# A two-layer graph network on one core: node tables laid out by group, query rows scattered by group during the clearing of their table

## The chip, the cores and the metric

The kernel runs on one core of one Trainium2 chip. The metric is device time in microseconds (us) of that core, the median of several runs. A profile is one more execution, recorded by the hardware profiler; its span goes from the first to the last instruction.

## What is computed

12500 nodes with 128 features, 200000 edges sorted by destination. The first layer is an attention layer over edges, the second a sum over neighbours with a small network. Cut to what matters (q, k, v have 8 heads of 16; every node also has a loop to itself):

```python
h = relu(layernorm(x))
q, k, v = (layernorm(h) @ W + b for each of q, k, v)
e = sum(q[dst] * k[src]) / sqrt(16)            # per edge and head, and per loop
alpha = softmax of e over the edges of a node
att = segment_sum(alpha * v[src], dst); 0 where a node has no edge
x1 = h + att @ Wo + bo;  x = x + x1 + gelu(layernorm(x1) @ W1 + bf1) @ W2 + bf2
h = relu(layernorm(x))
x = x + relu(((1 + eps) * h + segment_sum(h[src], dst)) @ gW1 + gb1) @ gW2 + gb2
```

## The kernel before

Five engines run programs written out by hand, with semaphores between them. Nodes are held in SBUF as `nodes`, 128 partitions by 98 columns; partition p has the nodes 98p to 98p+97. The work on nodes goes through 14 groups of 7 columns (`G`), two groups in each iteration of a loop (`PAIRS` = 7). Edges are held as 128 chunks of 1568 steps, handled in 98 batches of 16 steps (`B`); partition p walks through the edges 1568p to 1568p+1567.

*Stage A* (`group_a` on PE, DVE, ACT, `search` on GpSimd) normalizes each group, projects q, k and v (`take_qkv`, L1347 and L1348, adds the bias out of PSUM: k and v to a buffer that goes to the DRAM table `kv_tab`, q back into `nodes`), multiplies q by k for the loop scores (`loop_products`, L1353; `loop_scores`, L1360), and looks for the last edge of every node: a count over sampled destinations gives a block of 32 edges, GpSimd gathers that block (7 gathers per group from `dst_tab`, L612), and `last_edges` counts in it. GpSimd also adds a bias to the residual rows (L795) for the table `h0_tab`.

*The query table.* `q_edges` has a row of 128 values for each edge position. It is cleared to zero with 98 writes of 1 MB (`zero_fill`, L504, on SyncE's queue, two in flight). Then the query of each node is scattered to the row of its first edge, 98 scatters of 128 rows on GpSimd (`scatter_q`, L616); a node without edges gets an index out of bounds and is skipped. Each scatter reads a copy that ScalarE makes (`copy_q`, L978, L979). In stage B a scan on DVE (`fill`, L1459) carries each query down to the other edges of its node.

*Starts.* The index of a node's first edge is the last edge of the node before it, plus one. The node before lies mostly in the column before, but for the first column in another partition, so last edges are stored to `last_tab` in DRAM and read back shifted by one (L960, L963, L1424 to L1427). Two gathers from `last_tab` (`patch_raw`, `start_raw`) give what the first chunk positions need.

*Stage B* (`batch_b`): for each batch GpSimd gathers 16 times 128 rows of k and v (L612, `kv_tab`), SyncE loads the queries, DVE computes products (L1504), sums, scans for maximum and sum, and writes states. GpSimd may be two batches ahead: the gathers of batch n wait for `weighed_s` of batch n - 2. `batch_b(0)` (batches 0 and 1) stands ahead of `scatter_q` in GpSimd's program, the remaining 96 batches behind it. The stage begins on DVE when `edge_ready`, the first queries and `q_first` are there.

*Stages C to E*: attention output and feed-forward per group (C), the second edge sum (D, gathers from `h2_tab`), the last network and the store of the output (E).

```python
batch_b(0, True)                            # GpSimd, L827
for k in range(2):
    pool.wait_ge(q_zeroed[k], 16 * BPAIRS)
...
repeat(pool, PAIRS, scatter_q)
for k in range(2):
    pool.wait_ge(qs_out[k], GWAIT * PAIRS)
pool.wait_ge(place, PLACED)
gather(q_first[:], q_edges, q_row_i[:], q_first_in)
with pool.Fori(1, BPAIRS) as i:
    batch_b(i, False)
```

## Time and profile before

| what | value |
|---|---|
| median of 3 runs | 5002.62 us (5000.46 to 5006.18) |
| profiled execution, its own time | 5003.06 us |
| span of the profile | 5001.4 us |
| GpSimd (POOL) busy | 3474.5 us, 69% of the span |
| VectorE (DVE) busy | 2740.6 us, 55% |
| ScalarE (ACT) busy | 536.1 us, 11% |
| TensorE (PE) busy | 477.9 us, 10% |
| POOL's share of the chain that ended last | 35%, all of it gathers of L612 |
| stage A | about 34 to 291 us |
| clearing of the query table | 14 to 366 us |
| scatters of the queries | 367 to 493 us |
| stage B | 500 to 2507 us |

Read it with the stages in mind: the shares of the whole span are averages over stages that are limited by different engines. A line number in the profile is a line of the kernel; L612 and L616 are the helpers `gather` and `scatter`, so their rows are told apart by the tables that they name.

### The profile page before, as it was taken

How to read it: one execution, taken by the hardware profiler on the slowest of the kernel's cores; microseconds unless marked ns; L12 is line 12 of the kernel's file. 1: busy time of each engine (PE TensorE's matmuls, PEld its weight loads, DVE VectorE, ACT ScalarE, POOL GpSimd, SP SyncE). 2: the span in 40 equal slices, each digit the busy share in tenths (PEclk: the TensorE clock that was granted, in tenths of full speed). 3: DMA queues.
4: the chain of work that ended last, by engine and by line, in shares of the span. 5: the costliest groups of instructions: out<-in, count | busy, mean ns of one | idle time of the engine just before them, and what ended most of it. 6: DMA issues, size and time to landing. Idle time of an engine off the chain costs nothing.

```text
span 5001.4 us, 29558 instructions
## 1 busy us (share of the span) xinstructions
PE 477.9 (10%) x2293; PEld 343.9 (7%) x2293; DVE 2740.6 (55%) x7664; ACT 536.1 (11%) x1467; POOL 3474.5 (69%) x3619
## 2 busy tenths in 40 slices
PE   3610000000000000000068500000000000000005
PEld 2410000000000000000046400000000000000003
DVE  7820888888888888888868422222222222222224
ACT  3411000000000000000046400000000000000001
POOL 4547677777777777777655377777777777777766
PEclk8655555555555555555579755555555555555558
DMA  9991566666666666666633233333333333333334
GB/s 332 403 373 58 199 213 213 214 211 209 211 210 211 214 212 214 213 210 211 197 91 114 74 102 104 109 102 102 102 102 102 102 110 103 102 102 102 102 99 129
DMA packets 223032, 822.74 MB, mean 165 GB/s; under 512 B 66007, under 2 KB 80179, under 8 KB 172700
## 3 DMA queue, kind: packets, MB, share of 16 engines
q1 hardware_dynamic: 79467, 470.48, 24.9%
q0 software_dynamic: 139072, 331.82, 23.4%
q10 hardware_dynamic: 4466, 20.17, 1.0%
q14 instruction: 22, 0.18, 0.0%
q8 instruction: 5, 0.08, 0.0%
HBM read 461.59 MB, written 360.68 MB: 164 GB/s over the span
## 4 chain that ended last, share of the span: by engine, by line
POOL 35%; issue 22%; DVE 15%; DMA 13%; PE 4%; ACT 1%; DVEq 1%; POOLq 0%; ACTq 0%; SPq 0%
POOL arena L612 35%; DVE arena L1729 7%; DMA arena<-kv_tab,idx 5%; DMA arena<-h_tab,idx 4%; DVE arena L1575 3%; DMA states<-arena 2%; PE ps L1192 2%; PE ps L1203 1%; DVE arena L1522 1%; DVE ps L1561 1%; DMA arena<-states,node_idx 1%; DVE ps L1459 1%; DVE arena L1504 1%; DVE arena L1639 0%; PE ps L1224 0%
## 5 line engine op out<-in xcount | busy, mean ns | idle before, releaser
L612 POOL DMA_INDIRECT arena<-kv_tab,idx x1568 | 1497.7, 955 | 532.4 <-issue 484.8
L612 POOL DMA_INDIRECT arena<-h_tab,idx x1568 | 1490.7, 951 | 531.0 <-issue 476.3
L1729 DVE SCALAR_TENSOR_TENSOR arena<-arena 128x128 f32<-128x128 f32 x1568 | 555.0, 354 | 1445.6 <-DMA arena<-h_tab,idx 1393.4
L1459 DVE SCALAR_TENSOR_TENSOR ps<-ps,arena 128x128 f32<-128x128 f32 x1567 | 544.7, 348 | 4.0
L1575 DVE SCALAR_TENSOR_TENSOR arena<-arena,ps 128x128 f32<-128x128 f32 x1568 | 529.9, 338 | 0.5
L1504 DVE TENSOR_TENSOR arena<-arena,ps 128x512 f32<-128x512 f32 x392 | 266.5, 681 | 337.6 <-DMA arena<-kv_tab,idx 337.6
L612 POOL DMA_INDIRECT arena<-states,node_idx x196 | 196.0, 1000 | 149.4 <-DVE node_idx L1674 89.2
L1103 ACT COPY arena<-keep 128x16 f32 (+1 forms) x98 | 19.9, 204 | 1933.9 <-DVE arena L1729 1930.9
L1561 DVE TENSOR_TENSOR ps<-arena,ps 128x2048 f32<-128x2048 f32 x98 | 224.2, 2288 | 0.0
L1522 DVE TENSOR_REDUCE arena<-arena 128x128 f32<-128x2048 f32 x98 | 223.1, 2276 | 0.0
L1162 PE MATMUL ps<-arena,ones 128*128 128x512 f32 x4 | 3.8, 1098 | 2203.8 <-DVE arena L1481 2203.8
L1238 PE MATMUL ps<-arena 128*128 128x128 f32 x2 | 0.8, 486 | 2010.9 <-DVE arena L1729 2010.9
L612 POOL DMA_INDIRECT arena<-dst_tab,idx x98 | 96.2, 982 | 108.9 <-DVE idx L1401 83.2
L1162 PEld LDWEIGHTS ps<-arena,ones 128*128 128x128 f32 x4 | 1.2, 323 | 2205.5 <-DVE arena L1481 2204.5
L986 ACT COPY arena<-keep 128x16 f32 (+1 forms) x99 | 20.3, 205 | 1203.3 <-DVE arena L1575 1203.3
L1238 PEld LDWEIGHTS ps<-arena 128*128 128x128 f32 x2 | 0.5, 310 | 2011.1 <-issue 2011.1
L616 POOL DMA_INDIRECT q_edges<-arena,node_idx x98 | 96.3, 983 | 47.8 <-issue 27.4
L1466 DVE COPY ps<-q_first 128x128 f32<-128x128 f32 x1 | 0.3, 295 | 191.5 <-DMA q_first<-q_edges,q_row_i 191.5
L1203 PE MATMUL ps<-w,arena 128*128 128x128 f32 x784 | 98.8, 286 | 15.4 <-ACT arena L1063 15.4
L1155 PE MATMUL ps<-wqkv,arena 128*128 128x384 f32 x196 | 97.5, 667 | 23.9 <-ACT arena L951 23.9
L1203 PEld LDWEIGHTS ps<-w,arena 128*128 128x128 f32 x784 | 95.3, 202 | 25.5 <-ACT arena L1063 25.5
L1192 PE MATMUL ps<-arena,w 128*128 128x448 f32 x224 | 93.9, 555 | 1.2 <-ACT arena L1033 1.2
(222 smaller groups left out, 1877.3 us busy)
## 6 DMA issues: line engine op xcount, KB each, us to landing
states<-arena SPq DMA_DIRECT2D x98, 1152.0 KB, 4.9
q_edges<-arena SPq DMA_DIRECT2D x98, 1024.0 KB, 6.0
arena<-q_edges SPq DMA_DIRECT2D x98, 1024.0 KB, 7.5
states<-arena SPq DMA_DIRECT2D x98, 1024.0 KB, 4.1
arena<-kv_tab,idx POOLq DMA_INDIRECT x1568, 2.8
arena<-h_tab,idx POOLq DMA_INDIRECT x1568, 2.5
kv_tab<-arena ACTq DMA_DIRECT2D x14, 896.0 KB, 7.2
arena<-h_tab SPq DMA_DIRECT2D x28, 448.0 KB, 4.7
```

The lines of the kernel that those rows point to most:

```text
L612: pool.indirect_dma_start(to, None, tab, bass.IndirectOffsetOnAxis(ap=at, axis=0)).then_inc(done, 16)
L616: pool.indirect_dma_start(tab, bass.IndirectOffsetOnAxis(ap=at, axis=0), frm, None, bounds_check=EP - 1, oob_is_err=False).then_inc(done, 16)
L986: nc.scalar.copy(keepb[k], keep[:, bass.ds(n * B, B)]).then_inc(gates_set, 1)
L1155: nc.tensor.matmul(qkv_bank(j), hnT[:, j * HID:(j + 1) * HID], wqkv[:], start=True, stop=True)\
L1192: done = nc.tensor.matmul(halves(4 * k + 2 - 2 * (c % 2))[:, h, :], w1[:, c * P:(c + 1) * P], xT[k][:, h * HALF:(h + 1) * HALF], start=Tru ...
L1203: done = nc.tensor.matmul(two_banks(4 * k + 2)[1][j], gT[k][:, c, j * HID:(j + 1) * HID], w2[:, c, :], start=(c == 0), stop=(c == FC - 1))
L1459: nc.vector.scalar_tensor_tensor(q_now[:, b, :], q_now[:, (b - 1) % B, :], keepb[k][:, b:b + 1], qb[k][:, b, :], ALU.mult, ALU.add).then_i ...
L1504: done = nc.vector.tensor_tensor(keys, keys, q_now[:, b0:b1, :], ALU.mult)
L1522: nc.vector.tensor_reduce(score[:, :, 1:CW].rearrange("p h t -> p t h"), kvb[k][:, :, 0:HID].rearrange("p b (h d) -> p b h d", d=HD), AX.X ...
L1561: nc.vector.tensor_tensor(weighed.rearrange("p b (h d) -> p b h d", d=HD), kvb[k][:, :, HID:2 * HID].rearrange("p b (h d) -> p b h d", d=H ...
L1575: nc.vector.scalar_tensor_tensor(st[:, b, :], st[:, b - 1, :] if b else carried, keepb[k][:, b:b + 1], weighed[:, b, :], ALU.mult, ALU.add)\
L1729: nc.vector.scalar_tensor_tensor(rows[k][:, b, :], before, keepd[k][:, b:b + 1], rows[k][:, b, :], ALU.mult, ALU.add).then_inc(sum_s, 1)
```

## The change

1. **Layout.** Node index = group * 896 + partition * 7 + column in the group. All tables of nodes (`kv_tab`, `h0_tab`, `h2_tab`, x, the output) are addressed per group (`by_group`), so that a group is one contiguous block of 896 rows; the last group has 852 nodes and is moved in three pieces (`last_parts`). Loads of x, and stores of the output, need fewer DMAs; `x_tail` is gone.
2. **Clearing in order.** Each of the 98 writes clears 2048 consecutive rows of `q_edges` instead of 16 rows in each of the 128 chunks. SyncE counts landed writes in `zeroed`.
3. **Starts per pair of groups.** `place_starts` on DVE (eight small operations, two groups at once) computes first edges, `has_edges`, `sum_i` and `need_i`, the number of clearing writes that a group's scatter needs. The shift across partitions is a TensorE product with shift matrices (`shift`). The store to `last_tab` stays for the two patch gathers, the read back goes.
4. **Scatters per group.** GpSimd scatters group g - 5 at the end of `search` of group g, straight out of `nodes`; it loads `need_i` into a register and waits for `zeroed`. The last five groups follow the loop. `copy_q` is gone.
5. **Queries and products.** `take_qkv` adds the bias to q, k and v in one operation; ScalarE copies q into `nodes` (`keep_q`); the loop products run on GpSimd (`products`).
6. **Pipelining.** The first normalization of group g + 2 is done in group g. The loops of stage A are written out on all engines. Some preparation on DVE (`keep`, `pen`, `same_dst`) moves behind the last group; three memsets move from DVE to GpSimd.
7. **Stage B** has no prefetch any more: `batch_b(0)` stands behind scatters and `q_first`.

```diff
             def zero_fill(i, first):
                 for k in range(2):
                     if not first:
                         sp.wait_ge(q_zeroed[k], i * 16)
-                        settle(sp)
-                    sp.dma_start(by_step(q_edges)[:, bass.ds((i * 2 + k) * B, B), :], zeros)\
+                        sp.sem_inc(zeroed, 1)
+                    sp.dma_start(q_edges[bass.ds((i * 2 + k) * P * B, P * B), :].rearrange("(p b) f -> p b f", b=B), zeros)\
                         .then_inc(q_zeroed[k], 16)
...
+            def products(g, k, used):
+                pool.wait_ge(kv_set, g * G + G)
+                if used is not None:
+                    pool.wait_ge(scores_s, used)
+                settle(pool)
+                nc.gpsimd.tensor_tensor(qk[k], qkv_b[k][:, :, 0:HID], qkv_b[k][:, :, HID:2 * HID], ALU.mult)\
+                    .then_inc(qk_s, 1)
+            def scatter_q(g):
+                pool.wait_ge(starts_s, g // 2 + 1)
+                pool.wait_ge(q_set, g + 1)
+                rows_zeroed = pool.value_load(need_i[P - 1:P, g:g + 1], min_val=1, max_val=BATCHES)
+                pool.wait_ge(zeroed, rows_zeroed)
+                settle(pool)
+                for m in range(g * G, g * G + G):
+                    scatter(q_edges, start_i[:, m:m + 1], nodes[:, m, :], qs_out)
             def search(i, first):
...
                     nc.gpsimd.tensor_tensor(h0_bo[k], h0_b[k], bo[:].unsqueeze(1).to_broadcast([P, G, HID]), ALU.add)\
                         .then_inc(h0_s, 1)
+                    if not (first and k == 0):
+                        products(g - 1, 1 - k, None if g < 3 else g - 2)
                     pool.wait_ge(block_idx, i * 2 + k + 1)
                     for j in range(G):
                         gather(look[k][:, j, :].bitcast(I32), dst_tab, idx[k][:, j:j + 1], look_in[k])
-            repeat(pool, PAIRS, search)
+                    if g >= SCATTER_LAG:
+                        scatter_q(g - SCATTER_LAG)
+            for i in range(PAIRS):
+                search(i, i == 0)
+            products(2 * PAIRS - 1, 1, 2 * PAIRS - 2)
+            for g in range(2 * PAIRS - SCATTER_LAG, 2 * PAIRS):
+                scatter_q(g)
...
             pool.wait_ge(edge_ready, 1)
+            pool.wait_ge(qs_out, 16 * NODE_COLS)
+            pool.wait_ge(place, PLACED)
+            gather(q_first[:], q_edges, q_row_i[:], q_first_in)
...
-            batch_b(0, True)
-            for k in range(2):
-                pool.wait_ge(q_zeroed[k], 16 * BPAIRS)
...
+            repeat(pool, BPAIRS, batch_b)
...
                 for j in range(G):
                     m = g * G + j
                     dve.wait_ge(qkv_ps, m + 1)
-                    nc.vector.tensor_tensor(kv_b[k][:, j, :], qkv_bank(j)[:, HID:3 * HID], bqkv[:, HID:3 * HID], ALU.add)
-                    nc.vector.tensor_tensor(column(nodes, m), qkv_bank(j)[:, 0:HID], bqkv[:, 0:HID], ALU.add)\
-                        .then_inc(kv_set, 1)
+                    nc.vector.tensor_tensor(qkv_b[k][:, j, :], qkv_bank(j), bqkv[:], ALU.add).then_inc(kv_set, 1)
```

GpSimd's program from the end of stage A to the edge stage, before (arena is the SBUF area that holds buffers; the last row begins batch 2):

```order
L795 TENSOR_TENSOR arena<-arena,bo 128x896 [waits h0_set,h0_stored1]
L612 DMA arena<-dst_tab,idx 128x32 [waits block_idx]
...
L612 DMA arena<-last_tab,first_i 128x1 [waits last_io,place]
...
L612 DMA arena<-kv_tab,idx 128x256 [waits idx_set,edge_ready,kv_stored0,kv_stored1]
...
L616 DMA q_edges<-arena,node_idx 200704x128 [waits qs_copied,q_zeroed0,q_zeroed1]
L616 DMA q_edges<-arena,node_idx 200704x128 x6
...
L612 DMA q_first<-q_edges,q_row_i 128x128 [waits place,qs_out1,qs_out0]
...
L612 DMA arena<-kv_tab,idx 128x256 [waits weighed_s]
```

And the same engine now, one group of stage A from the sixth on:

```order
L834 TENSOR_TENSOR arena<-arena,bo 128x896 [waits h0_stored0,h0_set]
L815 TENSOR_TENSOR arena<-arena 128x896 [waits kv_set,scores_s]
L627 DMA arena<-dst_tab,idx 128x32 [waits block_idx]
L627 DMA arena<-dst_tab,idx 128x32 x6
L822 TENSOR_LOAD arena [waits q_set,starts_s]
L822 ISA x2
L631 DMA q_edges<-nodes,start_i 200704x128 [waits zeroed]
L631 DMA q_edges<-nodes,start_i 200704x128 x6
```

Scatters and a register load stand within each group; the first k and v gathers come behind `q_first`:

```order
L627 DMA q_first<-q_edges,q_row_i 128x128 [waits qs_out,edge_ready,place,kv_stored1,kv_stored0]
L627 DMA arena<-kv_tab,idx 128x256 [waits idx_set]
L627 DMA arena<-kv_tab,idx 128x256 x15
```

Here the prefetch of two batches has moved from ahead of the scatters to behind the last of them.

## Rows read from the trace of the kernel before

**Rows 1.** Table of windows: engine busy us (count), TensorE clock, DMA share, GB/s.

```profile
200.00:262.00 62.00, 35.11 (x123) 23.25 (x123) 52.66 (x213) 26.28 (x61) 30.22 (x27) 0.70 1.00 408
...
309.00:350.00 41.00, 0.00 (x0) 0.00 (x0) 0.00 (x0) 0.00 (x0) 30.23 (x32) 0.50 0.99 389
...
370.00:490.00 120.00, 0.00 (x0) 0.00 (x0) 0.00 (x0) 13.44 (x30) 91.68 (x94) 0.50 0.16 51
```

**Rows 2.** Line L504, clearing writes issued by six moments; first and last start us.

```profile
L504 SPq DMA_DIRECT2D q_edges<-arena x29: 332/332/432, 14.0 to 134.2; - x29
L504 SPq DMA_DIRECT2D q_edges<-arena x39: 332/332/432, 14.0 to 168.0; - x39
L504 SPq DMA_DIRECT2D q_edges<-arena x48: 332/332/432, 14.0 to 198.4; - x48
L504 SPq DMA_DIRECT2D q_edges<-arena x55: 332/332/432, 14.0 to 220.4; - x55
L504 SPq DMA_DIRECT2D q_edges<-arena x61: 332/332/432, 14.0 to 241.9; - x61
L504 SPq DMA_DIRECT2D q_edges<-arena x98: 332/332/432, 14.0 to 361.7; - x98
```

**Rows 3.** Timeline of GpSimd: start us, us, what, idle before.

```profile
88.88 1.03 POOL L612 DMA_INDIRECT arena<-dst_tab,idx  x1 [6.87 <-DVE idx L1401]
...
105.59 1.21 POOL L612 DMA_INDIRECT arena<-dst_tab,idx  x1 [6.38 <-DVE idx L1401]
...
367.25 1.03 POOL L616 DMA_INDIRECT q_edges<-arena,node_idx  x1 [18.22 <-DMA q_edges<-arena]
...
492.15 0.98 POOL L616 DMA_INDIRECT q_edges<-arena,node_idx  x1 [0.30 <-issue]
...
516.42 0.96 POOL L612 DMA_INDIRECT arena<-kv_tab,idx  x1 [20.20 <-DVE ps L1561]
```

**Rows 4.** Chain that ended last, edge stage: the same gather two batches apart.

```profile
564.21 1.17 POOL arena L612
...
604.59 1.18 POOL arena L612
```

**Rows 5.** Groups of GpSimd, 370 to 493 us: busy us, mean ns, idle before.

```profile
L616 POOL DMA_INDIRECT q_edges<-arena,node_idx x96 | 94.3, 982 | 29.2 <-issue 27.1 <-ACT node_idx L979 2.1
```

**Rows 6.** Groups by shape, 0 to 310 us, same columns.

```profile
L612 POOL DMA_INDIRECT arena<-dst_tab,idx x98 | 96.2, 982 | 108.9 <-DVE idx L1401 83.2 <-issue 24.2 <-ACT arena L242 1.5
...
L795 POOL TENSOR_TENSOR arena<-arena,bo 128x896 f32<-128x896 f32 x14 | 24.9, 1778 | 22.0 <-DMA gb<-in_L_gnn_b 21.7
```

**Rows 7.** Gathers from dst_tab, and line L1353: shortest, median, longest ns.

```profile
L612 POOL DMA_INDIRECT arena<-dst_tab,idx x98: 940/944/1567, 56.7 to 284.1; - x98
...
L1353 DVE TENSOR_TENSOR arena<-nodes,arena x14: 1055/1060/2455, 65.5 to 285.3; 128x896 f32<-128x896 f32 x14
```

**Rows 8.** Groups by shape, 0 to 310 us: DVE behind GpSimd's register load.

```profile
L1304 DVE CAST arena<-arena 128x1568 f32<-128x1568 int32 x1 | 1.0, 976 | 1.4 <-POOLq L771 1.4
```

**Rows 9.** Timeline of DVE, 5 to 12 us: two memsets ahead of the clearing.

```profile
5.64 4.75 DVE L1271 MEMSET nodes<- 32x5632 f32 x1 [1.23 <-issue]
10.89 1.76 DVE L1272 MEMSET arena<- 128x2048 f32 x1 [0.49 <-issue]
```

**Rows 10.** Timeline of GpSimd and DVE, patch gathers to first products.

```profile
300.10 0.94 POOL L612 DMA_INDIRECT arena<-last_tab,first_i  x1 [0.31 <-issue]
...
305.67 0.15 DVE L1431 CAST arena<-arena 128x1 f32<-128x1 int32 x1 [1.27 <-DMA arena<-last_tab,first_i]
...
309.37 0.94 POOL L612 DMA_INDIRECT arena<-kv_tab,idx  x1 [8.32 <-issue]
...
506.09 2.47 DVE L1504 TENSOR_TENSOR arena<-arena,ps 128x512 f32<-128x512 f32 x4
```

**Rows 11.** Table of windows, columns as in rows 1, attention stage.

```profile
2600.00:2800.00 200.00, 167.30 (x1014) 130.44 (x1013) 166.25 (x528) 135.27 (x203) 92.27 (x81) 0.97 0.36 108
```

**Rows 12.** Timeline of DVE, its last instruction.

```profile
4994.73 1.09 DVE L1748 TENSOR_TENSOR nodes<-ps,nodes 128x896 f32<-128x896 f32 x1 [6.83 <-PE ps L1260]
```

More of the change, by code:

```diff
@@ L286, in build @@
         hnT = cA.take(GW)
-        kv_b = cA.two(G, 2 * HID)
-        qk = cA.take(G, HID)
+        qkv_b = cA.two(G, 3 * HID)
+        qk = cA.two(G, HID)
         before_dst = cA.take(1).bitcast(I32)
@@ L329, in build @@
         last_s = sem("last_s")
+        zeroed = sem("zeroed")
+        shift_ps, starts_s = sem("shift_ps"), sem("starts_s")
         turns = sem("turns")
@@ L947, in group_a @@
                              lambda j: rstd1[:, j:j + 1], lambda j: nmr1[:, j:j + 1]).then_inc(hn_set, 1)
+                    if not last_group(g):
+                        relu0(g + 1, 1 - k, None if first and k == 0 else g)
                     if first and k == 0:
@@ L952, in group_a @@
                         .then_inc(hnT_set, 1)
-            repeat(act, PAIRS, group_a)
+                    if not (first and k == 0):
+                        keep_q(g - 1, 1 - k)
+                        store_kv(g - 1, 1 - k)
+                        store_h0(g - 1, 1 - k)
+            norm_root(act, lnA[0], 1)
+            norm_root(act, lnA[0], 2)
+            relu0(0, 0, None)
+            for i in range(PAIRS):
+                group_a(i, i == 0)
+            keep_q(2 * PAIRS - 1, 1)
             store_kv(2 * PAIRS - 1, 1)
@@ L1156, in group_a @@
                             .then_inc(qkv_ps, 1)
-            repeat(pe, PAIRS, group_a)
+            for i in range(PAIRS):
+                group_a(i, i == 0)
+            shift(PAIRS - 2, 2 * PAIRS - 1)
+            pe.wait_ge(starts_s, PAIRS - 1)
+            shift(PAIRS - 1, 2 * PAIRS - 1)
+            pe.wait_ge(prep, PREP_DIAG)
+            pe.wait_ge(search_s, 2 * PAIRS * 4)
+            nc.tensor.matmul(ps[:, 6, 0:P], ones[:], diag, start=True, stop=True).then_inc(last_rows, 1)
             pe.wait_ge(chunk_s, 1)
@@ L1368, in group_a @@
                                             spread(first_less_j[:, cols_g], P), ALU.is_ge).then_inc(starts, 1)
[L1369 to L1370 removed]
+                    dve.wait_ge(h0_set, g + 1)
                     settle(dve)
[L1372 to L1374 removed]
+                    norm_stats(dve, lnA[1], g + 1, [h0_b[k][:, j, :] for j in range(G)])
+                    if first and k == 0:
+                        dve.wait_ge(x_in, 16 * (1 + LAST_DMAS))
+                    if not (isinstance(i, int) and i == PAIRS - 1):
+                        stats0(g + 2)
+                    norm_scale(dve, lnA[1], g + 1, rstd1, nmr1)
+                    if not (isinstance(i, int) and i == PAIRS - 1):
+                        scale0(g + 2)
                     if k == 1:
@@ L1401, in group_a @@
                     nc.vector.tensor_scalar_add(idx[k][:, 0:G], block_f[:, cols_g], 0.0).then_inc(block_idx, 1)
-            repeat(dve, PAIRS, group_a, peel=2)
+            for g in range(2):
+                stats0(g)
+                scale0(g)
+            for i in range(PAIRS):
+                group_a(i, i == 0)
             take_qkv(2 * PAIRS - 1, 1, PAIRS * 16 - 16)
-            loop_products(2 * PAIRS - 1, 1)
-            loop_scores(2 * PAIRS - 1)
+            place_starts(PAIRS - 2)
             for k in range(2):
                 last_edges(2 * PAIRS - 2 + k, k, PAIRS - 1)
-            placed = [0]
+            place_starts(PAIRS - 1)
+            step(nc.vector.tensor_scalar(diag, ident[:], dst_f[:, STEPS - 1:STEPS], None, ALU.mult))
+            assert steps[0] == PREP_DIAG
+            step(nc.vector.memset(keep[:], 0.0))
+            step(nc.vector.tensor_tensor(keep[:, 1:STEPS], dst_f[:, 1:STEPS], dst_f[:, 0:STEPS - 1], ALU.is_equal))
+            step(nc.vector.tensor_scalar(pen[:], keep[:], -1.0, BIG, ALU.add, ALU.mult))
+            dve.wait_ge(last_rows, 1)
+            step(nc.vector.tensor_scalar(last_row, ps[:, 6, 0:P], dst_f[:, 0:1], None, ALU.is_equal))
+            step(nc.vector.tensor_tensor(same_dst[:], last_row, earlier[:], ALU.mult))
+            step(nc.vector.tensor_scalar(same_pen[:], same_dst[:], -1.0, BIG, ALU.add, ALU.mult))
+            for k in range(2):
+                loop_scores(2 * PAIRS - 2 + k, k)
+            placed = [PAIRS * PAIR_STEPS]
             def stage(ins):
```

335 lines of the change are left out of this document (169 added, 166 removed).

## The prediction

> **What bounds the kernel now.** I first read the page for the span: 5001.4 us, 1.7 us under the 5003.06 us of that execution; this in turn is 0.4 us above the median of 5002.62 us. Everything below is a difference against the profiled execution. Then I read the stretches in the table of windows [rows 1]. The reader should see three regimes ahead of the edge stage. While the groups are projected (200 to 262 us shown) DVE is busy 52.66 of 62 us and the DMA engines are at a share of 1.00. Later (309 to 350 us) only GpSimd does anything, yet DMA stays at 0.99: this is the clearing of the query table. From 370 to 490 us, 120 us long, DVE, TensorE and DMA (0.16) have next to nothing to do, and GpSimd issues query scatters. This last stretch is serial, and it is what the change aims at.
>
> The queue of SyncE tells how far the clearing is. It keeps two 1 MB writes in flight, so when it issues write n+2, write n has landed. Write 29 leaves at 134.2 us, write 39 at 168.0, 48 at 198.4, 55 at 220.4, 61 at 241.9, the 98th and last at 361.7 [rows 2]. GpSimd's first scatter follows at 367.25 after an 18.22 us wait for that, its 98th starts at 492.15, and the first gather for batch 2 of the edge stage at 516.42 [rows 3]. Batches 0 and 1 had been gathered before the scatters. From 516.42 on GpSimd never pauses: two batches take 604.59 - 564.21 = 40.4 us [rows 4]. So the whole edge stage is shifted rigidly by the moment at which GpSimd starts batch 2, and I compute only that moment.
>
> **Removed, added and moved.** (1) The 98 scatters leave the serial stretch. They cost 982 ns and a 0.30 us gap each, 9.0 us for a group of 7 [rows 5]. (2) They enter GpSimd's queue in the projection stage, five groups late, each group behind a register load and a wait for its part of the clearing. (3) GpSimd takes over the products of queries and keys from DVE. (4) The first two batches of gathers (40.4 us) move behind the scatters. (5) Starts come from a small matmul instead of a store and reload of last_tab.
>
> GpSimd's bill for one group: bias add 1.78 us; 7 gathers at 0.982 + 0.30 = 9.0 us [rows 6]; products, which no row shows on GpSimd, 1.8 us like the bias add of the same shape on the same engine (bounds: 1.06 and 2.46 us, the shortest and longest of the same operation on DVE [rows 7]); 7 scatters 9.0 us; register load and its checks. For this load the nearest row is DVE's wait of 1.4 us, which spans GpSimd's one register load of the program, its checks and a branch [rows 8]. So 0 to 1.4 us; I take 1.0, since most of that row is the same work, less the branch. With 0.3 us of gaps the sum is 1.78 + 1.78 + 8.97 + 8.97 + 1.0 + 0.3 = **22.8 us**. For the load the Trainium skill, "DMA: Bandwidth & Descriptors", section "Latency and other measured facts", states a floor of about 600 ns; by it each group would be 0.4 us shorter.
>
> Before, a group came every 105.59 - 88.88 = 16.7 us, set by DVE, and GpSimd waited 6.4 to 6.9 us in each [rows 3]. DVE now loses the products (1.06 us) and seven of its fourteen bias adds out of PSUM, and gains eight small operations for each two groups, so I estimate about 15 us a group. That paces groups 0 to 5; afterwards 22.8 us of GpSimd is more than 15 us of DVE, and DVE is covered. The same holds for ScalarE's copy of the queries. If this cover were gone (GpSimd much cheaper), DVE's 15 us would set the pace, which cannot push the end below the clearing.
>
> How much clearing does a group need? Destinations follow 12500 u^2, so node n has about 200000 sqrt(n/12500) edge rows before it, and a 1 MB write clears 2048 rows. Groups 0, 1, 2, 3, 4 need 27, 37, 46, 53, 59 writes, the last all 98. Their present moments are those of [rows 2], the last at 367. I shift them 3 us earlier, because GpSimd fills the index tiles while DVE clears a far smaller piece of nodes (it took 4.75 us) ahead of the source of the zeros (1.76 us) [rows 9], and two writes to x_tail vanish. Each scatter costs all DMA engines 120 x 0.16 / 93 = 0.2 us [rows 1], 1.4 us a group. This gives 133, 166.5, 198, 221.5, 244.5 us.
>
> Step by step: GpSimd is ready for scatter group 0 near 134. It is ready for group 1 at 157 but waits to 166.5, group 2: waits to 198, group 3: 221.5, group 4: 244.5. Then its own work rules: groups 5 to 8 start at 267.3, 290.1, 312.9, 335.7, the last ending at 344.7. One more product, 346.6. Groups 9 to 13 follow bare, 10.0 us each with the load: 396.6. The clearing ends at 367 - 3 + 11 x 1.4 - 10.5 = 369; the 10.5 us are the 32 moved gathers, 4.2 MB at about 400 GB/s, which no longer compete. The last group, starting at 387, does not wait. The prep moved behind the last group on DVE (masks, keep, pen, some 6 us) and the last_tab store with its 28-byte pieces are done long before 396.
>
> From the last scatter: two patch gathers 2.5 us; landing 2.6 us on the quiet engines (4.6 us now: 301.04 to 305.67); then DVE's chain to edge_ready and GpSimd's resumption, 305.67 to 309.37 = 3.7 us [rows 10]; q_first's gather 1.25 us. Batch 0's gathers start at 407 and batch 2's at 447.4. Batch 0's data lands near 430, and its 10.3 us until buffers come free (506.1 to 516.4 now [rows 3, 10]) end before 447, so DVE does not delay batch 2. **Shift: 516.4 - 447.4 = 69 us.**
>
> What stays: the attention stage is paced by TensorE, busy 167.30 of 200 us at a granted clock of 0.97 [rows 11], so two small x loads fewer are hidden there. If TensorE were faster, DVE (166.25) would be next. At the end the last store waits for DVE's operation of 4994.73 and covers two groups [rows 12]; one group is stored earlier now, 1 us. Sum: 5003.1 - 69 - 1 = **4933 us**.
>
> **Rivals.** *The clearing sets the end.* DMA is at its full share, so anything that makes it less efficient shows at once. If the scattered 512-byte writes cost 15% of its rate, it ends near 421 and the last scatters at 431: 4967 us. For: the share of 1.00. Against: the quiet stretch prices them at 0.2 us. Chance 0.10.
>
> *The port shared by DVE and GpSimd.* The scatters move from a stretch with DVE idle into one with DVE at 85%. Gathers there took 944 ns in the median but up to 1567 [rows 7], and DVE's product 2455 instead of 1060 ns beside a bias add. If each of the 63 scatters after the fifth group paid 0.6 us, the end would come 38 us later: 4971 us. Against: the mean of 98 gathers in this very stretch is 982 ns, 38 ns over the median. Chance 0.07. The Trainium skill, "SBUF — State Buffer", section "Who interferes with whom", says that DVE operations in a two-port mode lock GpSimd out of the port through which it writes descriptors. By that rule the scatters belong where DVE is idle; the trace agrees in kind, hardly in size.
>
> *Stalls in the unrolled code or in DVE's chain*, some 2 us a group over 14 groups: 4961 us. For: four engines lose their loops while DMA is saturated. Against: the first groups are straight-line now and show none. Chance 0.05.
>
> *Slower than before.* The clearing now writes one contiguous megabyte at a time instead of 128 distant pieces of 8 KB. If that cost rate, say through a few congested parts of DRAM, the cover would turn into the bound. The point of decision: batch 0 must start after 476, so the last scatter must end after 466 and the clearing after 456, 4.6 us a write on average instead of 3.6. At 5 us a write it ends at 500 and the kernel takes 5046 us. No row shows such a layout; the 408 GB/s of the present one [rows 1] speak for engines as the limit, not DRAM. Chance 0.05.
>
> *The change does nothing*: scatters stay behind the clearing, since each waits for too many writes. Then the end is the clearing plus all 98 scatters, less the moved prefetch: within 0.2% or so of now. The waits count by group, so only 0.03.
>
> *More gain*: no cost for load and products, scatters end at 384: 4920 us or a little less. 0.04.
>
> **Numbers.** The forecast holds with 0.66 and by the bounds of load, products and a part of the port's cost reaches from 4918 to 4950. For 8 in 10 I add most of the clearing, stall and port cases: 4915 to 4966. A measurement of this kernel can tell 0.2%, 10 us, from nothing. Faster: 0.66 + 0.10 + 0.07 + 0.05 + 0.04 = 0.92; same 0.03; slower 0.05.
>
> **What would show it.** Right: scatter groups on GpSimd about 23 us apart from 245 to 345 us, then 10 us apart; the last near 397, more than 10 us after the last clearing lands; the register load near 1 us; batch 2 near 447; 40.4 us for two batches, and attention, second edge stage and output unchanged. Wrong: the last scatter group waiting for zeroed, scatters above 1.2 us, GpSimd waiting for DVE's index after group 5, or a changed period of the edge stages.

## The result and the profile after

| | before | after |
|---|---|---|
| median of the runs | 5001.7 us | 4920.74 us |
| lowest to highest (4 runs each) | 5000.46 to 5006.18 us | 4920.10 to 4925.29 us |
| profiled execution, its span | 5003.06, 5001.4 us | 4920.1, 4918.2 us |

The median of the kernel before has one more run in it than the table ahead of the prediction. The ratio is 0.9838, 95% interval 0.9821 to 0.9856: the kernel is 81 us faster. The forecast was 4933 us, 12 us too high, inside the range of 4915 to 4966. Which step the 12 us belong to is the subject of what follows.

First the clearing in SyncE's queue: the writes issued by three moments, and the two last waits for it.

```profile
L517 SPq DMA_DIRECT2D q_edges<-arena x29: 332/332/3726, 18.6 to 128.4; - x29
L517 SPq DMA_DIRECT2D q_edges<-arena x62: 332/332/3726, 18.6 to 242.0; - x62
L517 SPq DMA_DIRECT2D q_edges<-arena x98: 332/332/3726, 18.6 to 369.2; - x98
L522 SPq EVENT_SEMAPHORE  x2: 17/17/17, 371.9 to 375.0; - x2
```

Against [rows 2] the clearing is ahead at first: the first write leaves 4.6 us later (18.6 in place of 14.0), the 29th 5.8 us earlier (128.4 in place of 134.2), and by 242 us 62 writes are issued where there were 61. Its last write is issued 7.5 us later, and has landed at 375.0.

GpSimd's timeline: start, duration, what, and the idle time before it with its releaser. The rows are the first scatters of groups 0, 1, 2, 3, 4, 5, 6, 8 and 13, the last scatter, q_first, and the first gathers of batches 0 and 2.

```profile
130.91 1.03 POOL L631 DMA_INDIRECT q_edges<-nodes,start_i  x1 [0.30 <-issue]
164.75 1.02 POOL L631 DMA_INDIRECT q_edges<-nodes,start_i  x1 [12.54 <-SPq L516]
194.63 1.02 POOL L631 DMA_INDIRECT q_edges<-nodes,start_i  x1 [8.10 <-SPq L516]
218.19 1.02 POOL L631 DMA_INDIRECT q_edges<-nodes,start_i  x1 [1.67 <-SPq L516]
240.29 1.02 POOL L631 DMA_INDIRECT q_edges<-nodes,start_i  x1 [0.30 <-issue]
262.49 1.02 POOL L631 DMA_INDIRECT q_edges<-nodes,start_i  x1 [0.30 <-issue]
284.59 1.02 POOL L631 DMA_INDIRECT q_edges<-nodes,start_i  x1 [0.30 <-issue]
327.75 1.02 POOL L631 DMA_INDIRECT q_edges<-nodes,start_i  x1 [0.30 <-issue]
376.48 0.98 POOL L631 DMA_INDIRECT q_edges<-nodes,start_i  x1 [0.30 <-issue]
384.21 0.98 POOL L631 DMA_INDIRECT q_edges<-nodes,start_i  x1 [0.30 <-issue]
...
392.85 0.94 POOL L627 DMA_INDIRECT q_first<-q_edges,q_row_i  x1 [5.11 <-issue]
394.10 0.95 POOL L627 DMA_INDIRECT arena<-kv_tab,idx  x1 [0.30 <-issue]
434.12 0.95 POOL L627 DMA_INDIRECT arena<-kv_tab,idx  x1 [0.30 <-issue]
```

The reader should see three things. The scatter groups wait for the clearing at groups 1, 2 and 3 (12.54, 8.10 and 1.67 us), then never again; they follow each other at 22.1 us (284.59 - 262.49). The last group begins 1.5 us after the clearing has landed: an idle time of 0.30 us before 376.48 looks as if GpSimd alone set the end, but the clearing is only 1.5 us behind that. And batch 2 starts at 434.12 in place of 516.42 [rows 3]: a shift of 82.3 us, which is nearly the whole result (the two spans differ by 83.2 us).

The groups of GpSimd from 0 to 400 us by shape (busy us, mean ns, idle time before), and the line of the register load (shortest, median, longest ns):

```profile
L627 POOL DMA_INDIRECT arena<-dst_tab,idx x98 | 99.6, 1017 | 43.9 <-issue 26.0 <-DVE idx L1466 17.0 <-SPq L516 0.6
L631 POOL DMA_INDIRECT q_edges<-nodes,start_i x98 | 98.5, 1005 | 51.1 <-issue 27.9 <-SPq L516 22.9 <-SPq L522 0.3
...
L815 POOL TENSOR_TENSOR arena<-arena 128x896 f32<-128x896 f32 x14 | 29.5, 2111 | 1.6 <-DVE arena L1412 1.5
```

```profile
L822 POOLq TENSOR_LOAD <-arena x14: 423/998/1328, 121.4 to 370.1; - x14
```

A scatter takes 1005 ns (982 in [rows 5]), a gather 1017 (982 in [rows 6]), the product 2111. The register load lasts 998 ns in the median, close to the 1.0 us forecast, yet the idle time before the scatter that follows it is 0.30 us, as everywhere.

The table of windows, columns as in [rows 1]:

```profile
200.00:262.00 62.00, 31.60 (x85) 19.09 (x86) 33.99 (x135) 22.31 (x50) 49.76 (x44) 0.64 1.00 384
309.00:350.00 41.00, 1.79 (x6) 1.43 (x6) 12.31 (x26) 0.31 (x2) 33.34 (x30) 0.51 0.99 372
```

Between 200 and 262 us DVE falls from 52.66 to 33.99 us of work and GpSimd rises from 30.22 to 49.76; with its gaps of 0.30 us GpSimd has hardly any time left there, and it sets the pace in DVE's place. The DMA engines are as full as before (1.00) but move 384 GB/s in place of 408.

The edge stage keeps its period. In the chain that ended last, the same gather of one batch and of the next starts at 482.08 and 502.33: 20.25 us, half the 40.4 us of [rows 4].

### The profile page after: what moved, and what is told of

It reads as the page before. It is cut to its first block, busy times and chain, and to the rows that moved or that the text cites. A ratio compares the mean times of both kernels' runs of the same rounds, so it can differ in the third digit from the quotient of the medians.

```text
span 4918.2 us, 28859 instructions
## 1 busy us (share of the span) xinstructions
PE 483.5 (10%) x2321; PEld 345.3 (7%) x2321; DVE 2723.5 (55%) x7600; ACT 531.6 (11%) x1453; POOL 3509.0 (71%) x3637
## 3 DMA queue, kind: packets, MB, share of 16 engines
q0 software_dynamic: 139072, 331.82, 23.6%
## 4 chain that ended last, share of the span: by engine, by line
POOL 39%; issue 22%; DVE 14%; DMA 12%; PE 4%; ACT 1%; DVEq 1%; POOLq 0%; ACTq 0%; SPq 0%
POOL arena L627 39%; DVE arena L1803 8%; DMA arena<-kv_tab,idx 5%; DMA arena<-h_tab,idx 5%; DMA states<-arena 2%; DVE arena L1649 2%; PE ps L1239 2%; DVE arena L1596 1%; PE ps L1250 1%; DMA arena<-states,node_idx 1%; DVE ps L1635 1%; DVE arena L1578 1%; DVE arena L1713 1%; PE ps L1271 0%; DVE arena L251 0%
## 5 line engine op out<-in xcount | busy, mean ns | idle before, releaser
L631 POOL DMA_INDIRECT q_edges<-nodes,start_i x98 | 98.5, 1005 | 51.1 <-issue 27.9
L627 POOL DMA_INDIRECT arena<-dst_tab,idx x98 | 99.6, 1017 | 43.9 <-issue 26.0
L1195 PE MATMUL ps<-wqkv,arena 128*128 128x384 f32 x196 | 108.4, 717 | 116.6 <-ACT arena L988 60.5
L1250 PE MATMUL ps<-w,arena 128*128 128x128 f32 x784 | 99.4, 288 | 15.4 <-ACT arena L1093 15.4
L1041 ACT COPY arena<-arena 128x128 f32<-128x128 f32 x98 | 39.8, 406 | 311.6 <-DVE arena L1656 311.6
```

The costliest lines, as they stand in the source:

```text
L627: pool.indirect_dma_start(to, None, tab, bass.IndirectOffsetOnAxis(ap=at, axis=0)).then_inc(done, 16)
L631: pool.indirect_dma_start(tab, bass.IndirectOffsetOnAxis(ap=at, axis=0), frm, None, bounds_check=EP - 1, oob_is_err=False).then_inc(done, 16)
L1195: nc.tensor.matmul(qkv_bank(j), hnT[:, j * HID:(j + 1) * HID], wqkv[:], start=True, stop=True)\
L1250: done = nc.tensor.matmul(two_banks(4 * k + 2)[1][j], gT[k][:, c, j * HID:(j + 1) * HID], w2[:, c, :], start=(c == 0), stop=(c == FC - 1))
```

## The experiments

The first four went to a chip on which the kernel before took 5807 us, its extra time in the loops of the edge stage; totals of one group of runs therefore stand only against the kernel before on the same chip, and times inside the first 450 us are read from each trace.

**1. All scatters behind the last search.**

```
-SCATTER_LAG = 5
+SCATTER_LAG = 14
```

> The changed kernel, with every scatter group after the last search (the distance between a search and its scatter group is 14 groups in place of 5; waits, clearing, products and layout as in the changed kernel). My theory (GpSimd's own work and the end of the clearing bind together, and it matters little when GpSimd does a scatter group, as long as its work isn't held up): the searches then go at DVE's pace, 14 groups of 16.2 us from 42 us, to 269 us; 14 scatter groups of 9.0 us from there would end at 395, the last not before 375.0 + 9.0 = 384. Scatters end at 395 in place of 385.2, the kernel takes about 4930 us (4924 to 4934). Rival A (it is the interleaving with the searches that pays, scatters run beside DVE's work for nothing): the scatters add their whole 14 x 9 us behind the old end of the searches, and the kernel comes out near the one before, 5000 us. Rival B (the clearing alone sets the end): the scatters end at 384 and the kernel takes 4919 to 4921 us.

Measured: 0.9904 of the kernel before (0.9869 to 0.9938). The last scatter started at 413.56, not near 395, since the clearing landed at 404.1. The table of windows of this run shows why:

```profile
310.00:340.00 30.00, 0.00 (x0) 0.00 (x0) 0.00 (x0) 0.00 (x0) 22.75 (x24) 0.50 0.62 232
340.00:365.00 25.00, 0.00 (x0) 0.00 (x0) 0.00 (x0) 0.00 (x0) 19.21 (x20) 0.50 0.47 178
```

DMA is busy 0.62 and 0.47, where the changed kernel has 0.99: SyncE did not issue its clearing writes in time, and single instructions of its clearing loop took up to 713 ns, where they take at most 81 in the changed kernel. So either packed scatters hold SyncE up, or this chip does, as it stretches other loops. The same kernel was run again on another chip:

> The kernel with every scatter group behind the last search once more, because on the chip of the first time SP's loop of clearing writes itself stalled (DMA busy 0.62 and 0.47 between 310 and 365 us), which the changed kernel never shows. My theory: with the clearing kept busy it lands at 375 to 385 us, and GpSimd's 14 groups of 9.0 us from 273.6 us end at 400: the kernel is 12 to 18 us slower than the changed one. Rival (scatters packed behind the searches slow the clearing itself, as the first run showed): the clearing lands at 404 again, the last scatter ends at 414, 28 us slower.

Measured on a chip on which the kernel before takes 5006 us: 0.9854 (0.9838 to 0.9869), 4931.64 us, 7 to 8 us above the changed kernel's share of the kernel before, where 12 to 18 were expected. The clearing landed at 372.8. Below are SyncE's last waits, then GpSimd's first and last scatter and its first gather of batch 2.

```profile
L522 SPq EVENT_SEMAPHORE  x2: 17/17/17, 369.7 to 372.8; - x2
```

```profile
266.61 1.04 POOL L631 DMA_INDIRECT q_edges<-nodes,start_i  x1 [0.17 <-issue]
...
392.45 0.98 POOL L631 DMA_INDIRECT q_edges<-nodes,start_i  x1 [0.31 <-issue]
...
442.49 0.95 POOL L627 DMA_INDIRECT arena<-kv_tab,idx  x1 [0.30 <-issue]
```

So packed scatters by themselves do not slow the clearing more than spread ones. What stalled SyncE on the first chip stays open: on that same chip the DMA engines were full to the end of the clearing in experiment 2, where no scatter runs beside it. The searches end 7 us earlier than I took, the last scatter starts at 392.45, and batch 2 comes 8.4 us later than in the changed kernel. Some nine tenths of what the overlap gives is thus to be had without interleaving scatters with searches: what matters most is that GpSimd works while the clearing goes on, not when.

**2. No overlap at all.** As above, and each scatter group waits for the whole clearing.

```
-                rows_zeroed = pool.value_load(need_i[P - 1:P, g:g + 1], min_val=1, max_val=BATCHES)
-                pool.wait_ge(zeroed, rows_zeroed)
+                pool.wait_ge(zeroed, BATCHES)
```

> As the run with every scatter group after the last search, but each scatter group also waits for the whole clearing, as the kernel before did (the layout by groups, the products on GpSimd and the flat clearing blocks of the changed kernel stay). My theory: the scatters start when the clearing has landed, 366 to 375 us, and last 14 x 9.0 = 126 us, to 492 to 501 us, 107 to 116 us later than in the changed kernel; the kernel takes 5028 to 5037 us, which is 26 to 35 us more than the kernel before, whose gathers of the first batches stood ahead of its scatters. Rival (the gain comes from the flat blocks and the new front, not from the overlap): 4921 to 4950 us.

Measured: 1.0033 (1.0013 to 1.0052), slower than the kernel before, so the overlap is the whole gain. The loss is 17 us, where 26 to 35 were expected, because the clearing, alone on the DMA engines, ended early (line of SyncE's last waits, then GpSimd's first and last scatter, then the window 309 to 350 us):

```profile
L522 SPq EVENT_SEMAPHORE  x2: 17/17/17, 348.9 to 351.4; - x2
```

```profile
352.50 1.04 POOL L631 DMA_INDIRECT q_edges<-nodes,start_i  x1 [77.88 <-issue]
...
477.53 0.98 POOL L631 DMA_INDIRECT q_edges<-nodes,start_i  x1 [0.30 <-issue]
```

```profile
309.00:350.00 41.00, 0.00 (x0) 0.00 (x0) 0.00 (x0) 0.00 (x0) 0.00 (x0) 0.50 1.01 423
```

This prices what the scatters take from the clearing: it lands at 351.4 without them and at 375.0 with 91 of them beside it, 23.6 / 91 = 0.26 us each. The forecast had 0.2. With the 82 to 83 scatters that started before the clearing ended in the repeated run above it is (372.8 - 351.4) / 82 = 0.26 again. These landings are from different chips; the changed kernel's own, run twice, differ by 0.3 us (375.0 and 374.7).

**3. The kernel before, with flat clearing blocks.**

```
-                    sp.dma_start(by_step(q_edges)[:, bass.ds((i * 2 + k) * B, B), :], zeros)
+                    sp.dma_start(q_edges[bass.ds((i * 2 + k) * P * B, P * B), :].rearrange("(p b) f -> p b f", b=B), zeros)
```

> The kernel before with one line changed: each clearing write fills 2048 rows in a row of the table, in place of 16 rows of every one of the 128 chunks. The same bytes and the same number of writes. My theory: the layout costs nothing, the clearing ends at 366 us as before and the kernel takes 5000 to 5004 us. Rival A (my forecast's slower rival): contiguous blocks cost rate, the clearing ends tens of us later and the kernel with it, 5030 us and more. Rival B: the 8 us by which the clearing ended later in the changed kernel (375.0 in place of 366.9) come from the layout; then this kernel is 5010 us.

Measured: 1.0000 (0.9985 to 1.0014). A window of this run and its first scatter:

```profile
200.00:262.00 62.00, 36.35 (x132) 24.23 (x131) 52.43 (x205) 26.45 (x63) 31.12 (x28) 0.72 0.99 403
```

```profile
370.35 1.03 POOL L616 DMA_INDIRECT q_edges<-arena,node_idx  x1 [17.34 <-DMA q_edges<-arena]
```

403 GB/s in this window, where [rows 1] has 408, and 409 in the next (262 to 309 us; 407 in the kernel before): flat megabytes cost no rate that shows. That refutes the rival on the slower side. Its milder form, that the layout explains the 8 us by which the clearing ends later in the changed kernel, keeps at most 3 of them: the first scatter is 3.1 us later than 367.25 [rows 3], and that on a chip where one instruction of SyncE's clearing loop took up to 717 ns (72 in the kernel before's own profile). The total can't tell 3 us from nothing.

**4. Products back on DVE.**

```
-                    if not (first and k == 0):
-                        products(g - 1, 1 - k, None if g < 3 else g - 2)
```

and `loop_products` in DVE's loop, ahead of `loop_scores`.

> The changed kernel with the 14 products of keys and queries back on DVE; GpSimd keeps bias adds, gathers and scatters. GpSimd's cycle is then 22.1 - 2.1 = 20.0 us. If GpSimd's own work set the end of the scatters (step of my sum: nine groups at the long cycle), they end 9 x 2.1 = 19 us earlier less what the clearing's pace takes back, down to the clearing's end 375.0 plus one group, 384: a gain of 1 us at most. My theory: both bind together, so 4919 to 4921 us. Rival (only GpSimd's work counts, the clearing's end is not in the way): 4900 to 4908 us. Rival (DVE is near its limit in this stage): its period of 16.2 us grows by 1.8 us in the first groups, and the kernel gets 2 to 10 us slower.

Measured: 0.9886 (0.9853 to 0.9919), with stalls in SyncE's loop as well (clearing landed at 383.2), so this run decides nothing. Again, beside the repeated run above:

> The kernel with the products back on DVE once more, for the same reason (SP's loop stalled there as well, and the clearing landed at 383 us). My theory (the clearing at 375 sets the last group of scatters): within 2 us of the changed kernel. Rival A (GpSimd's work alone sets it): 12 us faster and more. Rival B (DVE's 1.8 us more per group reach the end): 3 to 10 us slower.

Measured: 0.9833 (0.9818 to 0.9848), 4923.48 us, where the changed kernel has 0.9835 to 0.9838. GpSimd's waits for SyncE and for DVE's index, first in this kernel, then in the changed kernel run again (total, times, longest), and last the first scatter of group 12 and the first gather of batch 2:

```profile
POOL q_edges L631 <- SPq L516: 40.5, 7, 14.2
POOL arena L627 <- DVE idx L1471: 27.9, 6, 7.7
```

```profile
POOL q_edges L631 <- SPq L516: 21.8, 5, 10.9
POOL arena L627 <- DVE idx L1466: 16.9, 5, 7.0
```

```profile
367.30 0.98 POOL L631 DMA_INDIRECT q_edges<-nodes,start_i  x1 [2.36 <-SPq L516]
...
434.29 0.95 POOL L627 DMA_INDIRECT arena<-kv_tab,idx  x1 [0.30 <-issue]
```

The clearing landed at 375.7. 29.5 us of work taken from GpSimd give nothing: waiting for the clearing rises by 18.7 us, and waiting for DVE's index takes the rest (27.9 us in place of 16.9). Batch 2 still starts at 434.3. That shows the bound: the last stretch of the clearing. The last wait stands before group 12, whose part is 95 of the 98 writes; from there two groups of 9.0 us lead to the last scatter, and group 13 doesn't wait again, since the last three writes have landed by then (375.7).

**5. The thresholds as constants.**

```
-                rows_zeroed = pool.value_load(need_i[P - 1:P, g:g + 1], min_val=1, max_val=BATCHES)
-                pool.wait_ge(zeroed, rows_zeroed)
+                pool.wait_ge(zeroed, NEED[g])
```

with `NEED` holding this input's 14 values. The changed kernel itself ran beside it.

> The changed kernel itself once more, as the base of the three runs beside it: the chip of the first four experiments took 5807 us for the kernel before, its extra time in the loops of the edge stages, so their totals stand only against each other. Expected: the same first 450 us as in the first profile (last scatter near 384, batch 2 near 434), and 81 us less than the kernel before, whatever that one takes here.

> The changed kernel with the 14 loads of a threshold into a register of GpSimd's queue replaced by the constants that they hold for this input (27, 37, 46, 53, 59, 64, 70, 74, 79, 83, 87, 91, 95, 98). My theory (the load of 1.0 to 1.3 us runs while the DMA instructions issued before it still run on GpSimd, so it costs nothing): no change, within 3 us of the changed kernel, the last group of scatters at the same 375 us. Rival (each load stands in GpSimd's path, as my forecast had it at 1.0 us): 9 groups of 1.0 us earlier, with the clearing's end as the floor; the searches' period falls from 22.1 to 21.1 us.

Measured: 0.9835 (0.9819 to 0.9852) for the changed kernel, 0.9831 (0.9814 to 0.9847) with constants. GpSimd's scatter groups 5, 6 and 8 with constants:

```profile
263.34 1.02 POOL L632 DMA_INDIRECT q_edges<-nodes,start_i  x1 [0.30 <-issue]
...
285.43 1.02 POOL L632 DMA_INDIRECT q_edges<-nodes,start_i  x1 [0.30 <-issue]
...
328.60 1.02 POOL L632 DMA_INDIRECT q_edges<-nodes,start_i  x1 [0.30 <-issue]
```

The steps are 22.1 us, then 43.2 us for two, exactly as with the loads (262.49, 284.59, 327.75). The load of 1 us costs nothing. That it runs in GpSimd's queue while the gathers issued ahead of it still run on the engine is the reading that fits, since the idle time behind it is 0.30 us with the load and without.

**6. Seven groups of distance in place of five.** `SCATTER_LAG = 7`.

> The changed kernel with 7 groups in place of 5 between a search and its scatter group. GpSimd then never waits for the clearing in groups 1 to 3 (12.5, 8.1 and 1.7 us in the changed kernel), and issues the same instructions. My theory (clearing and GpSimd bind together, and fewer scatters before 240 us let the clearing run ahead, more after it hold it back): GpSimd reaches its last group at about 372 us, the clearing lands at 373 to 377, the kernel within 4 us of the changed one. Rival A (the waits for the clearing in groups 1 to 3 cost time to the end): 10 to 22 us faster. Rival B (scatters packed behind the searches slow the clearing more than spread ones): the clearing lands at 385 and later, 10 us or more slower.

Measured: 0.9834 (0.9817 to 0.9850). Waits for the clearing fell from 21.8 to 9.6 us, the clearing landed at 375.5, and the last scatter started where it did. The first row is the first scatter of group 12:

```profile
367.45 0.98 POOL L631 DMA_INDIRECT q_edges<-nodes,start_i  x1 [3.53 <-SPq L516]
...
384.21 0.98 POOL L631 DMA_INDIRECT q_edges<-nodes,start_i  x1 [0.31 <-issue]
...
434.39 0.95 POOL L627 DMA_INDIRECT arena<-kv_tab,idx  x1 [0.30 <-issue]
```

The total is as expected. The waits did not vanish, they moved: groups 1 to 3 no longer wait, groups 10, 11 and 12 do (2.77, 3.26 and 3.53 us), so once more the pace of the clearing near its end decides.

**7. Keys ahead of the last group.** A distance of 7 groups, and GpSimd's order changed at the end (`kv_rows` issues gathers of keys and values):

```
-SCATTER_LAG = 5
+SCATTER_LAG = 7
+HELD, EARLY = 1, 9
...
+            kv_rows(0, 0, EARLY)
+            for g in range(2 * PAIRS - HELD, 2 * PAIRS):
+                pool.wait_ge(zeroed, BATCHES)
...
+            kv_rows(0, EARLY, EARLY + 2)
             gather(q_first[:], q_edges, q_row_i[:], q_first_in)
```

> A distance of 7 groups, and GpSimd's order changed at the end of the scatters: the two patch gathers and nine key-and-value gathers of batch 0 are issued before the last scatter group, which waits for the whole clearing anyway; the q_first gather stands behind two more of them, then the rest of batches 0 and 1 as before. If GpSimd has about 10 us free before the clearing ends, these 11.3 us of gathers cost 0 to 4 us there and take 11.3 + 2.6 us off the path behind the last scatter; its wait of 5.1 us before q_first is filled by 2.5 us more. My theory: the last scatter ends at 384 to 390, batch 2 starts 10 to 16 us earlier than in the changed kernel, the kernel is 8 to 16 us faster than that. Rival (DVE's chain from q_first through batch 0 to the release of its buffer becomes the bound, or the clearing is held back by the gathers): 0 to 5 us.

Measured: 0.9836 (0.9819 to 0.9852), nothing gained, where 8 to 16 us had been expected.

```profile
385.41 0.95 POOL L628 DMA_INDIRECT arena<-kv_tab,idx  x1 [5.34 <-issue]
...
396.68 1.04 POOL L632 DMA_INDIRECT q_edges<-nodes,start_i  x1 [0.30 <-issue]
```

Groups 9 to 12 wait for their own part of the clearing, so GpSimd reaches the patch gathers only at 377.8. Its free time lies in those waits, not behind group 12; the moved gathers and a 5.34 us wait for the patch chain then stood ahead of the last group, which could have started when the clearing landed, at 376.8.

**8. The waits filled.** A distance of 7 groups again. The two patch gathers and six gathers of batch 0 are spread over those waits, and the thresholds of the last four groups are loaded ahead of them (`scatter_rows` is a scatter group that is handed its threshold):

```
-SCATTER_LAG = 5
+SCATTER_LAG = 7
+HELD, EARLY = 4, (0, 3, 3, 0)
...
+            held = [pool.value_load(need_i[P - 1:P, g:g + 1], min_val=1, max_val=BATCHES)
+                    for g in range(2 * PAIRS - HELD, 2 * PAIRS)]
...
             gather(start_raw, last_tab, first_i[:, 0:1], patch_in)
+            scatter_rows(2 * PAIRS - HELD, held[0])
...
+            for n in range(1, HELD):
+                kv_rows(0, b0, b0 + EARLY[n])
+                b0 += EARLY[n]
+                scatter_rows(2 * PAIRS - HELD + n, held[n])
```

> A distance of 7 groups; GpSimd's waits for the clearing's pace at the end (2.8, 3.3 and 3.5 us ahead of groups 10, 11 and 12 with that distance) are filled: the two patch gathers stand before group 10, three key-and-value gathers of batch 0 before group 11 and three before group 12; the thresholds of the last four groups are loaded into registers ahead of them. Behind the last scatter stand two more gathers, q_first, then the rest of batches 0 and 1. My theory: the last scatter ends at 385 to 387 as before, since the clearing sets it; 2.6 us of patch gathers, 6 x 1.25 = 7.5 us of batch 0 and the 5.1 us of waiting before q_first leave the path: batch 2 starts at 420 to 422 in place of 434, and the kernel is 10 to 14 us faster than the changed one. Rival (the release of batch 0's buffer by DVE, chained to q_first, comes later than GpSimd's 421): 5 to 10 us. Rival (the gathers slow the clearing): 0 to 5 us.

Measured: 4908.47 us, 0.9803 (0.9790 to 0.9817): faster than both kernels, 97.7 us under the kernel before beside it and some 15 us under the changed one (which in its own runs was 81 and 84 us under, on other chips; with products on DVE, which was no different, it took 4923.48 us on this one).

```profile
341.37 0.99 POOL L628 DMA_INDIRECT arena<-last_tab,first_i  x1 [0.30 <-issue]
...
353.02 0.99 POOL L628 DMA_INDIRECT arena<-kv_tab,idx  x1 [0.32 <-issue]
...
379.84 0.98 POOL L632 DMA_INDIRECT q_edges<-nodes,start_i  x1 [1.35 <-SPq L523]
...
391.42 0.94 POOL L628 DMA_INDIRECT q_first<-q_edges,q_row_i  x1 [0.30 <-issue]
...
422.67 0.95 POOL L628 DMA_INDIRECT arena<-kv_tab,idx  x1 [0.30 <-issue]
```

Batch 2 starts at 422.67, 11.5 us earlier than in the changed kernel, where 12 to 14 had been expected; the rest of the 15 us lies behind that and was not looked into. The last group now visibly waits for the clearing (1.35 us, released by SyncE's last wait at 378.9), which landed 4 us later than in the changed kernel.

**9. Both.** Filled waits with products on DVE and twelve gathers of batch 0 in place of six, `HELD, EARLY = 4, (0, 3, 4, 5)`.

> The kernel with filled waits, and the products back on DVE as well, so that 14 x 2.1 = 29 us of GpSimd's work go where GpSimd waits for the clearing; 12 gathers of batch 0 in place of 6 stand before the last three scatter groups (3, 4 and 5 of them). My theory: the clearing lands at 376 to 381 us, the last scatter ends at 388 to 391, two gathers, q_first and the last two of batch 0 follow, batch 1 starts 7.5 us earlier than in the run before, batch 2 at 415 to 418 in place of 422.7, and the kernel takes 0.978 to 0.979 of the kernel before, 5 to 8 us less than with filled waits alone. Rival A (batch 2 waits for DVE's release of batch 0's buffer, which hangs on q_first and so on the last scatter): 0 to 4 us. Rival B (DVE, slower with the products, delays the searches and with them the last groups): slower than with filled waits alone.

Measured: 0.9865 (0.9841 to 0.9890), on a chip on which the kernel before takes 5832 us and SyncE's loop stalls again (DMA busy 0.73 between 309 and 350 us, single instructions up to 1425 ns). The longest wait on GpSimd's way was this:

```profile
367.39 0.99 POOL L628 DMA_INDIRECT arena<-last_tab,first_i  x1 [24.21 <-DMA last_tab<-arena]
```

`last_tab`, stored by ScalarE at 357 us (345 in the changed kernel), was late, and the patch gather held scatter group 10 behind it. Whether DVE's added products or the chip made it late, and whether this version beats the one with filled waits elsewhere, stays open. It does show the risk of the filled order: a gather moved up brings its own wait.

## Why the prediction was right, and where it was off

*The serial stretch goes, and the edge stage shifts rigidly.* Right. Shift 82.3 us in the trace, 83.2 us in the span, 81 in the medians; the period of the edge stage is unchanged. The run without overlap gives back all of it.

*GpSimd's bill for a group, 22.8 us.* Measured 22.1, later 21.6. Nearly the right sum, with one wrong term: the register load was put in GpSimd's path at 1.0 us. It does last 998 ns, but costs 0 (experiment 5); the row it was priced from [rows 8] shows a load ahead of which GpSimd had nothing running. This is the term that was mis-sized: nine groups of it (5 to 13), and with it the five bare groups at 10.0 us, which took 9.0 but for the first (10.7, with one slow scatter, see the last section). The Trainium skill, "DMA: Bandwidth & Descriptors", section "Latency and other measured facts", has a floor of about 600 ns for such a load; the shortest here is 423 ns, so the measurement decides, and neither number reached the time. Smaller errors went the other way: the product 2.11 us in place of 1.78, gathers and scatters about 0.03 us over 0.98 in the mean.

*The last scatter ends at 396.6, GpSimd's own work sets it, the last group doesn't wait.* Here the prediction was off by 11.4 us, and incomplete in the name of the bound. The last scatter ended at 385.2. Group 4 started at 240.29 where 244.5 was forecast, since its part of the clearing had landed earlier: 4.2 of the 11.4 us. The other 7.2 lie in the nine groups behind it: 9.0 us of loads that cost nothing, less 1.8 us of smaller errors. GpSimd then reaches the last group at 376.5, and the clearing has landed at 375.0. The sign "wrong: the last scatter group waiting" did not come, but only by 1.5 us: in the changed kernel both bounds lie that close together. Experiments 4 and 6 show that the clearing is the one that can't be passed: taking work or waits from GpSimd moves neither the last scatter nor batch 2.

*The clearing ends at 369.* It landed at 375.0. The forecast had 15.4 us for 77 scatters; it was 23.6 us for 91, since each costs 0.26 us in place of 0.2 and GpSimd is further on by then. Without the scatters its own terms (3 us for the earlier front, 10.5 for the 32 gathers that left) give 353.5, and experiment 2 landed at 351.4, so these two held to 2 us together. They were not separated: the front was 5.8 us ahead by the 29th write, as DMA moved 384 GB/s in place of 317 from 14 to 75 us, and against that stands some 3% less rate (392 GB/s from 75 to 140 us of experiment 2, where the kernel before had 403), which by experiment 3 isn't the flat blocks' doing and stays unexplained. A slip of the forecast changed nothing: by its own terms group 0's part of the clearing comes at 131.2, not at 133, and GpSimd was taken to be ready at 134.

*Batch 0 is 10.4 us behind the last scatter.* Measured 8.9 (385.2 to 394.1): from the end of the second patch gather to DVE's first operation on it 1.4 us passed in place of 2.6. *Prefetch of two batches*: 40.0 us in place of 40.4. *The tail*: 83.2 less 82.3 leaves 0.9 us, forecast 1, but that is luck in part. Behind DVE's last operation the span is 2.0 us shorter (6.7 us in [rows 12], 4.7 now), and 1.1 us of the shift is lost between batch 2 and there.

Summed: 11.4 us of the last scatter, 1.5 us of the chain and 0.4 us of the prefetch are the 13.3 us between the two shifts.

*The rivals.* "More gain" had 4920 us, from no cost for load and products: the number came out to a microsecond, by luck: the product did cost more, the clearing was ahead at group 4, and the chain behind the last scatter was 1.5 us shorter. It had been given 0.04, too little, because the load's row spans a load alone. The clearing that sets the end had been given 0.10 as a loss; it is the bound, at no loss. The port of DVE and GpSimd costs 23 ns a scatter at most, not 600 (below). The slower side is refuted by experiment 3. The forecast also counts from one profiled execution, 5003.06 us, which is 1.4 us above the median.

## What to carry to other kernels

When a serial stretch is moved under a saturated one, price what it takes from the saturated resource first (here 91 scatters cost 24 us of clearing), because that end, plus the last pieces that depend on it, is the new floor; below it, cheaper work on the moved engine only becomes waiting. A register load in an engine's queue need not cost its duration: here 14 loads of 1 us behind seven gathers or scatters each cost nothing. Once waits remain, fill each with work that was to come later, in the size of that wait and where it lies, and look first at what the moved work waits for itself: spread over the waits it gave some 11 to 15 us, in one block ahead of the last group nothing.

## What the runs showed of the hardware

Two engines slow each other at single instructions. DVE's comparison of two SBUF tiles, L1481, took 3.20 us while GpSimd worked on its product, and the scatter that ran beside it and DVE's next operation took 2.63 us in place of 0.98. DVE's timeline, then GpSimd's:

```profile
337.09 3.20 DVE L1481 TENSOR_TENSOR keep<-arena 128x1567 f32<-128x1567 f32 x1
340.32 0.98 DVE L1482 TENSOR_SCALAR pen<-keep 128x1584 f32<-128x1584 f32 x1
```

```profile
336.53 2.10 POOL L815 TENSOR_TENSOR arena<-arena 128x896 f32<-128x896 f32 x1
338.80 2.63 POOL L631 DMA_INDIRECT q_edges<-nodes,start_i  x1 [0.17 <-issue]
```

With the products on DVE the same comparison took 1.79 us:

```profile
L1487 DVE TENSOR_TENSOR keep<-arena x1: 1792/1792/1792, 330.9 to 330.9; 128x1567 f32<-128x1567 f32 x1
```

The Trainium skill, "SBUF — State Buffer", section "Who interferes with whom", has both engines sharing a port pair; the trace agrees in kind. Over all 98 scatters the mean rose from 982 to 1005 ns only, and 17 of these 23 ns are the one scatter of 2.63 us, so it is no reason to keep scatters away from DVE.

Two of the four chips of the experiments ran the kernel before 16% slower in total (5807 and 5832 us). Experiment 3, the kernel before but for its clearing, has its first scatter at 370.35 on one of them, so that its first 370 us are nearly unchanged, while some instructions of SyncE's clearing loop took 0.7 us in place of 0.06. Why these chips differ is not shown. A comparison of totals across chips would have read this as an effect of the edit.
